# Forty SBUF places in place of a ring of six for the row blocks of a bfloat16 expert stage

## The reference

```python
# x: (8, 512, 256); E = 8 experts, K = 2 chosen per token, I = 256
normed = (xf * rsqrt(mean(xf * xf) + 1e-5) * norm_weight).astype(bfloat16)
scores, idx = top_k(logits, 2);  w = softmax(scores)
p1 = einsum('bsh,eoh->bseo', normed, mlp1_weight) + mlp1_bias
g, lin = minimum(p1[..., 0::2], 7.0), clip(p1[..., 1::2], -7.0, 7.0)
act = g * sigmoid(1.702 * g) * (lin + 1.0)
p2 = einsum('bsei,ehi->bseh', act, mlp2_weight) + mlp2_bias
out = xc + sum over the two chosen experts of w * p2
```

## Time and profile before

| | |
|---|---|
| time, median of 3 runs | 2828.16 us (2823.35 to 2835.19) |
| the profiled execution: its time | 2800.93 us |
| the profiled execution: its span | 2799.2 us |
| TensorE busy, share of the span | 80% |
| VectorE, ScalarE, GpSimd busy | 57%, 48%, 26% |
| mean granted TensorE clock, of full speed | 0.88 |
| first load of the expert blocks issued | 1448.60 us from the start of the span |
| first load of result rows issued | 1687.85 us |

### The profile page before, as it was taken

One profiled execution on the slowest core, in us unless ns is written; L12 is line 12 of the kernel. 1 busy time (PEld: TensorE's weight loads), 2 busy tenths in 40 slices (PEclk: granted clock), 3 DMA queues, 4 the chain that ended last, 5 costly groups with the idle time before them and its releaser, 6 DMA issues. The chain is left out here.

```text
span 2799.2 us, 43146 instructions
## 1 busy us (share of the span) xinstructions
PE 2243.0 (80%) x13073; PEld 1724.5 (62%) x13073; DVE 1590.1 (57%) x4481; ACT 1330.7 (48%) x2654; POOL 731.5 (26%) x828
## 2 busy tenths in 40 slices
PE   4899999999999998687636670588888889687783
PEld 3788888888888887365534450255555555474662
DVE  4556656565566663567554446377677678562225
ACT  3345545454554543454344344277767678410231
POOL 5111111111111110335343442012222212217442
PEclk8899999999999999898766665699999999868897
DMA  5710100010000000322312224122222122122446
GB/s 107 155 28 8 33 1 1 8 33 1 0 8 3 1 0 9 79 54 51 58 58 67 71 65 149 53 77 71 70 66 68 42 68 79 50 66 105 126 138 237
DMA packets 209472, 165.36 MB, mean 59 GB/s; under 512 B 108320, under 2 KB 167376, under 8 KB 209296
## 3 DMA queue, kind: packets, MB, share of 16 engines
q1 hardware_dynamic: 190832, 120.71, 16.5%
q0 software_dynamic: 14240, 38.35, 4.4%
q10 hardware_dynamic: 4224, 4.19, 0.4%
HBM read 91.07 MB, written 72.11 MB: 58 GB/s over the span
## 5 line engine op out<-in xcount | busy, mean ns | idle before, releaser
L630 PE MATMUL psum_o<-w_s,hid_s 128*128 128x256 f32 x3072 | 384.0, 284 | 19.1 <-ACT hid L434 19.1
L616 PE MATMUL psum_h<-xn2T_s,w_s 128*128 128x512 f32 x1536 | 391.0, 405 | 6.8 <-ACT hid L434 3.7
L630 PEld LDWEIGHTS psum_o<-w_s,hid_s 128*128 128x128 f32 x3072 | 371.8, 188 | 27.0 <-issue 19.1
L433 ACT ACTIVATE hid_s<-psum_h,b 128x512 fp32r<-128x512 f32 x256 | 176.5, 690 | 391.9 <-PE psum_h L616 376.5
L616 PEld LDWEIGHTS psum_h<-xn2T_s,w_s 128*128 128x128 f32 x1536 | 284.4, 191 | 88.8 <-ACT hid L434 21.8
L2011 DVE CUSTOM_DVE_ANT_0 ra_z<-ra_psum_s,ra_rhat 128x128 f32<-128x128 f32 (+3 forms) x512 | 226.4, 484 | 154.2 <-PE ra_psum_s L2113 140.3
L1952 ACT ACTIVATE ra_z<-ra_z,ra_nm 128x128 f32<-128x128 f32 (+3 forms) x512 | 245.1, 560 | 0.0
L1877 POOL TENSOR_SCALAR_AFFINE_SELECT ra_z<-ra_z 128x512 f32<-128x512 f32 x128 | 81.6, 637 | 481.0 <-DVE ra_z L2040 481.0
L2125 PE MATMUL ra_psum_p<-ident,ra_z 128*128 128x128 f32 x1280 | 185.7, 297 | 1.3 <-ACT ra_pt L1944 1.3
L517 DVE TENSOR_TENSOR hid_s<-hid,hid_s 128x1024 fp32r<-128x1024 f32 x128 | 156.1, 1224 | 43.2 <-ACT hid L434 42.2
L1944 ACT ACTIVATE ra_pt<-ra_psum_p 128x1024 f32<-128x1024 f32 x128 | 131.2, 1025 | 94.5 <-PE ra_psum_p L2125 94.5
(11 more groups left out here) (364 smaller groups left out, 4229.4 us busy)
## 6 DMA issues: line engine op xcount, KB each, us to landing
ex_slots<-blank SPq DMA_DIRECT2D x1, 10296.0 KB, 33.8
ex_zT<-ex_slots SPq DMA_DIRECT2D x39, 264.0 KB, 3.0
ex_rows<-ex_slots SPq DMA_DIRECT2D x8, 1056.0 KB, 9.3
w<-in_L_tok_w SPq DMA_DIRECT2D x8, 1024.0 KB, 7.5
be_back_y<-be_results SPq DMA_DIRECT2D x8, 1024.0 KB, 5.7
ra_scratch<-ra_hi SPq DMA_DIRECT2D x32, 256.0 KB
ra_scratch<-ra_lo SPq DMA_DIRECT2D x32, 256.0 KB
ra_q_st<-ra_scratch SPq DMA_DIRECT2D x128, 64.0 KB, 1.8
```

Of the source, the lines that this page charges most:

```text
L433: act.activation(hid_s[:, 0, m, :], psum_h[:, m % 2, :], ACT.Gelu, bias=b1[:, m:m + 1])
L616: mm = pe.matmul(psum_h[:, m % 2, :], w1_s[:, w_part, k, m * P:(m + 1) * P], xn2T_s[:, x_part, k, :], start=(n == 0 and k == 0), stop=(n = ...
L630: mm = pe.matmul(psum_o[:, t // 2, (t % 2) * D:(t % 2 + 1) * D], hid_s[:, h_part, m, t * P:(t + 1) * P], w2_s[:, w_part, m, :], start=(n = ...
```

## The change

`zs` gets 40 places (`BLOCKS`) in place of 6, one for each block. SyncE's wait for the result scatter of block `j-6` goes. In its place, from the seventh load on, it waits until load `j-6` has landed, so that no more than six loads are under way and the six load semaphores count on as before. GpSimd and TensorE read the block's own place. The ring of 4 result tiles stays.

```diff
--- before.py
+++ after.py
@@ -1514,8 +1514,8 @@
 
         sem = Semaphores(nc, ctx, "be_")
 
-        RING, YRING = 6, 4
-        zs = sb("zs", [P, RING, 2, ROWLEN])
+        ABOARD, YRING = 6, 4
+        zs = sb("zs", [P, BLOCKS, 2, ROWLEN])
         zsT = sb("zsT", [P, 2, DK, WIDE], BF16)
         lin = sb("lin", [P, 2, IK, WIDE])
         gate, act_b = sb("gate", [P, 2, IK, WIDE]), sb("act_b", [P, 2, IK, WIDE])
@@ -1528,7 +1528,7 @@
         bank = [ctx.enter_context(nc.psum_tensor(f"be_bank{n}", [P, T], F32)) for n in range(8)]
         psum_z = bank[0][:, :].bitcast(BF16)[:, 0:2 * DK * P]
 
-        zs_loaded = [sem(f"zs_loaded{n}") for n in range(RING)]
+        zs_loaded = [sem(f"zs_loaded{n}") for n in range(ABOARD)]
         zs_turned, zsT_ready, p1_done = sem("zs_turned"), sem("zsT_ready"), sem("p1_done")
         gated, lin_taken, lin_ready, act_ready = sem("gated"), sem("lin_taken"), sem("lin_ready"), sem("act_ready")
         high_ready, low_ready = sem("high_ready"), sem("low_ready")
@@ -1545,11 +1545,10 @@
         @block_ctx.sync
         def _(sp):
             for j in range(BLOCKS):
-                if j >= RING:
-                    done, value = sent_before(j - RING)
-                    sp.wait_ge(done, value)
+                if j >= ABOARD:
+                    sp.wait_ge(zs_loaded[j % ABOARD], 16 * (j // ABOARD))
                 at = sp.value_load(row_at[0:1, j:j + 1], min_val=0, max_val=DUMMY + (E - 1) * WIDE)
-                sp.dma_start(zs[:, j % RING, :, :], slots[ds(at, WIDE), :].rearrange("(s p) n -> p s n", p=P)).then_inc(zs_loaded[j % RING], 16)
+                sp.dma_start(zs[:, j, :, :], slots[ds(at, WIDE), :].rearrange("(s p) n -> p s n", p=P)).then_inc(zs_loaded[j % ABOARD], 16)
             for j in range(BLOCKS - YRING, BLOCKS):
                 done, value = sent_before(j)
                 sp.wait_ge(done, value)
@@ -1564,7 +1563,7 @@
             for j in range(BLOCKS):
                 pool.wait_ge(y_ready, j + 1)
                 for s in range(2):
-                    pool.indirect_dma_start(results, bass.IndirectOffsetOnAxis(ap=zs[:, j % RING, s, WORDS:WORDS + 1].bitcast(I32), axis=0),
+                    pool.indirect_dma_start(results, bass.IndirectOffsetOnAxis(ap=zs[:, j, s, WORDS:WORDS + 1].bitcast(I32), axis=0),
                                             ys[:, j % YRING, s, :], None).then_inc(y_sent[j % YRING], 16)
 
         @block_ctx.scalar
@@ -1651,13 +1650,13 @@
             find(0)
             for i in range(BLOCKS + 3):
                 if i < BLOCKS:
-                    pe.wait_ge(zs_loaded[i % RING], 16 * (i // RING + 1))
+                    pe.wait_ge(zs_loaded[i % ABOARD], 16 * (i // ABOARD + 1))
                     if i >= 1:
                         pe.wait_ge(zsT_ready, i)
                     for s in range(2):
                         for k in range(DK):
                             at = (k * 2 + s) * P
-                            mm = pe.transpose(psum_z[:, at:at + P], zs[:, i % RING, s, 0:WORDS].bitcast(BF16)[:, k * P:(k + 1) * P], ident16[:, :])
+                            mm = pe.transpose(psum_z[:, at:at + P], zs[:, i, s, 0:WORDS].bitcast(BF16)[:, k * P:(k + 1) * P], ident16[:, :])
                     mm.then_inc(zs_turned, 1)
                 if 0 <= i - 1 < BLOCKS:
                     j = i - 1
```

## The result

| | before | after |
|---|---|---|
| median of the runs, us | 2826.91 (4 runs, 2823.35 to 2835.19) | 2751.23 (4 runs, 2746.92 to 2755.59) |
| profiled execution, us | 2800.9 | 2746.9 |
| first load of a block to first load of results, us | 239.3 | 150.4 |
| period of a block, transposes of block 5 to those of block 39, us | 6.00 | 3.39 |

The ratio is 0.9728, 95% interval 0.9699 to 0.9758: faster by 76 us, where 110 were forecast. The range held, by 0.8 us at its upper end; the point was 33 us too low. In the new kernel each line of the stage has a number one less than before (L1551 the load, L1566 the scatter, L1618 the first linear row, L1659 the transposes, L1670 the first layer).

A forecast was written before the change was run, and what follows sets the result against it. The six-place `zs` ring was taken to bound the stage: scatter, landing and next load did not fit, 6.00 us a block. Removing the wait gives 107 us, the stage's end 3: 2828.2 - 110 = 2718 us, range 2700 to 2752.

The forecast's parts named there:

- The new wait at 0: SyncE's added wait for load `j-6` to land: over when reached, 0 to 1 us at the start, taken as 0.
- the swinging clock: TensorE's clock swings between levels; half the blocks at each gives 31 us more, 2749 us; chance 0.09.
- 34 x (6.00 - 2.85) = 107 us: SyncE's 34 waits for result scatters go; the block period falls from 6.00 to 2.85 us, saving 107 us.
- the undisturbed loop: Loop through TensorE and VectorE without slowing by GpSimd: 5.44 us for two blocks, 2.72 a block.
- the warm stretch: First six blocks of the old trace at the risen clock, read as the new order: bias matmuls 2.58 and 2.86 us apart.
- The slowing of VectorE by GpSimd: Old L1623 taking 0.63 us, not 0.427, beside a scatter; paid every time, VectorE's block would be 2.85 us.
- the two-port rule: Skill rule cited under the first rival: a two-port VectorE form and a GpSimd instruction shut each other out of SBUF.
- The end of the stage: Block 39's transposes to first load of results: 20.5 us becomes 17.1, 3 us off, or 0 if GpSimd's backlog stays.
- The second rival: TensorE's clock swings: 2749 us with half the blocks at each level, 2780 us if low throughout; chance 0.09.
- The first: GpSimd and VectorE hold each other up: 3.36 us a block, 17 us more, 2735 us; chance 0.10.
- third: The load did not bind alone; something else holds each block for 6 us: no change, 2828 us; chance 0.03.
- fourth: Ring of `ys` stops ScalarE at L1598 as scatters land late: period 6.4, 14 us slower, 2842 us; chance 0.02.

The follow-up runs named there:

- the repeat: The changed kernel once more, nothing left out, on the chip of the 264-column fill run: 2743.22 us, ratio 0.9703.
- the last run: Changed kernel plus a waited-for GpSimd fill of 8 columns after every second indirect scatter, both expert stages; another chip: 2693.48 us, ratio 0.9593.

## Why the prediction was right or wrong

**The bound was read rightly.** The ring of six was what held the stage: any slack (twelve places, or one for each block) takes the 34 waits away. Issue of 40 loads in "some 47 us": 48.5. The new wait at 0: right. The range held by luck: its upper end, 2752, was set by the swinging clock, which isn't what took the time, and the signs named for the forecast (2.85 a block, first load of results at about 1577, scatters at 1.15 us in the mean) were missed: 3.39, 1615.1 and 1.09.

**The term that failed** is "34 x (6.00 - 2.85) = 107 us". The 6.00 was right. The 2.85 is 3.39: 34 x 2.61 = 89 us, 18 less. It failed in both directions at once. What the engines allow is 2.73, as the runs with plain stores and the one with fills behind every second scatter show, so the choice above the undisturbed loop wasn't needed. And none of the rows read showed the delay that makes 3.39 of it. The prediction took the spacing of the warm stretch for the whole stage, but its three bias matmuls start at 1459.55 to 1464.99, and GpSimd's first scatter at 1464.31: nearly the whole stretch lies before the disturbance can begin. And they came from an execution that had late signals nowhere.

**The slowing of VectorE by GpSimd** didn't come. L1622, the old L1623, kept its median:

```profile
L1622 DVE TENSOR_SCALAR be_lin<-be_lin x40: 426/427/609, 1471.6 to 1602.4; 128x512 f32<-128x512 f32 x40
```

427 ns, as in the earlier trace rows, at 86 of 115 us of VectorE's time. The scatters were 1.09 us in the mean, 1.38 where one begins during L1613, as foretold. The Trainium skill, SBUF — State Buffer, section Who interferes with whom, says that `tensor_tensor`, the form of L1613, has no two-port mode, but contends with GpSimd's reads when both its inputs are in SBUF; the row of 1.38 agrees with that, and not with the two-port rule that the prediction named. The slowing doesn't explain the loss: both the run with the small fills and the one with plain stores have VectorE at 87 of 93 us and no lateness.

**The end of the stage** was to give 3 us. It is 20.4 us (1594.7 to 1615.1) after 20.5: nothing, the lower end that was named, for the reason named there. GpSimd still had a backlog, six scatters 1.27 us apart up to 1613.56.

**The clock** from block 5 to block 39 was 1.00 with plain GpSimd stores, with half of the scatters, with the fill of 8 columns and with the second scatter held back, and 0.94 in the kernel after, with its pauses of TensorE. The second rival isn't what made 3.39: the run with the second scatter held back has 3.35 at clock 1.00. Nor do the traces bear out, for idles this short, the section that it named (the Trainium skill, TensorE: Matmul & The Clock Gate, section A second HAM failure mode: psum-queue depth-cycling): the order goes round banks with idles of 0.17 to 0.30 us, at clock 1.00.

**The rivals.** The first named the right engine and nearly the right time (2735 us; 2751 measured), by the wrong mechanism: the scatters weren't all 1.38 us long. That GpSimd is near its limit matters in another way: two scatters of 1.09 (74.45 / 68) and two gaps of 0.30 make 2.79 a block, just over the loop's 2.73, so that scatters can queue up into chains. That this is how the chains begin is argued, not shown: with the small fill GpSimd's own sum is 2 x 1.01 + 0.30 + 0.40 = 2.72, hardly less. The third and fourth fell.

**Median and profile.** The median of before stood 27 us over its profile. The prediction subtracted its sum from the median and let the 27 stand, rightly: they lie in the second group of scatters and in front of the stage, and the kernel after pays both. By terms the forecast was 110 and the stage gave 89; the medians differ by 76 us in the result and by 84 in the repeat. The remaining 5 to 13 us lie in the spread of those two places and aren't settled further.

**What stays open.** Shown: TensorE's news arrives up to 3.2 us late when GpSimd's indirect scatters follow each other in chains of more than two, in five different kernels of the first expert stage, and up to 45.8 us late in the second. In executions that have late signals elsewhere it isn't late in the first stage with plain stores, with half the scatters, or with a fill of 264 columns behind each scatter. Not shown: which path is blocked (that TensorE's own matmuls come apart by 1.5 us in the second stage says that it isn't only the way of the finished signal); why the execution of before, and perhaps a whole chip, is free of it; whether the fill or the wait for it releases it; and whether a small fill behind every second scatter does. A fill without a wait, a wait for a signal from another engine, and the kernel after on the chip of the last run weren't tried.

## What to carry to other kernels

Take a ring's wait away only after you have worked out every engine's own sum in the new period, and look hardest at an engine whose sum lies within a few per cent of it: here GpSimd, at 2.79 us against 2.73, ran its scatters in chains, and the delay beside them cost 18 us of the 107 forecast. Where consumers of TensorE idle on "remote" while GpSimd sends indirect DMAs without pause, try a waited-for GpSimd instruction between them: behind each one it removed the delay here, at a price that ate the gain; a tiny one behind every second is worth a try, and has to be measured against the kernel without it on the same chip. A stretch of the old trace shows the new order only if every engine has reached the load that it will have there. And look through a second profile before you trust one: here the first was of an execution that had no late signals at all.

## What was not expected of the hardware

- A finished group of matmuls was noticed by ScalarE and VectorE up to 3.0 us late in the kernel after (45.8 us in its second expert stage) while GpSimd's indirect DMAs ran in chains of more than two; 0.04 us otherwise. The executions of before and of the last run show none of it.
- A fill of 264 columns with a wait behind each indirect DMA took the late signals away at a gap of 0.61 us; the same gap without a fill, or a semaphore wait already met, didn't. The period fell from 3.44 to 3.04 us and the time stayed (2743.22 and 2739.95 us).
- A fill of 8 columns with a wait behind two indirect DMAs cost 0.10 us for a pair.
- A plain DMA cost GpSimd 0.54 us for 128 rows and 0.72 for 256 (24.38 / 34), an indirect one of 128 rows 0.96 to 1.40.
